# Low parts of the expert weights, taken in five conv steps of VectorE instead of three

## The reference, cut to what matters

```python
def _L0_attn_ref(...):                       # "the conv part" of the kernel
    p = hidden_states @ in_proj_w.T
    h, gate = p[..., :I], silu(p[..., I:])   # I = 256
    h = (causal grouped conv of h, 4 taps) + conv_b
    h = h * gate                             # the gated product
    hn = _layernorm(h, ln_g, ln_b)
    m = silu(hn @ fc_w.T + fc_b) @ cproj_w.T + cproj_b
    return (m + h) @ out_w.T
x = _layernorm(x + _L0_attn_ref(x, ...))     # "the first norm"
...
def _L0_ffn_ref(x, gate_w, w1, w2, w3):      # 8 experts, top 2 of them per token
    scores = softmax(x2d @ gate_w.T); top_scores, sel = top_k(scores, 2)
    for e in range(8):                       # on the rows sent to expert e
        h = silu(xe @ w1[e]) * (xe @ w3[e]); out += h @ w2[e]
x = _layernorm(x + _L0_ffn_ref(x, ...))
```

## Time and profile before

| | |
|---|---|
| time, median of 3 runs | 378.95 us (378.64 to 382.75) |
| the profiled execution | 379.13 us, its span 377.3 us |
| TensorE busy in the span | 330.8 us (88%) |
| VectorE | 262.0 us (69%) |
| ScalarE | 210.4 us (56%) |
| GpSimd | 174.6 us (46%) |
| mean granted clock of TensorE | 0.965 |
| chain that ended last | TensorE 63%, VectorE 10%, issue 5%, ScalarE 3%, GpSimd 3% |

### The profile page before, as it was taken

One profiled execution on the slowest core, in us unless ns is written; L12 is line 12 of the kernel. 1 busy time (PEld: TensorE's weight loads), 2 busy tenths in 40 slices (PEclk: granted clock), 3 DMA queues, 4 the chain that ended last, 5 costly groups with the idle time before them and its releaser, 6 DMA issues.

```text
span 377.3 us, 8518 instructions
## 1 busy us (share of the span) xinstructions
PE 330.8 (88%) x2540; PEld 302.3 (80%) x2540; DVE 262.0 (69%) x857; ACT 210.4 (56%) x430; POOL 174.6 (46%) x234
## 2 busy tenths in 40 slices
PE   4799889966875999999985999999988999999990
PEld 1788778956764999888974788888787999999990
DVE  3558887875872567768774589987796867667741
ACT  2266556735522355445448678887467667667340
POOL 0014577673464345886579666643311342244200
PEclk9899999998897899999999899999999999999996
DMA  8980001021132433322501300000000000000001
GB/s 276 432 341 1 16 29 39 29 66 28 50 87 77 147 99 103 126 58 58 156 23 31 111 2 0 3 3 0 2 3 1 2 14 17 14 14 1 14 16 31
DMA packets 17033, 23.71 MB, mean 63 GB/s; under 512 B 3424, under 2 KB 14176, under 8 KB 16208
## 3 DMA queue, kind: packets, MB, share of 16 engines
q1 hardware_dynamic: 13712, 17.97, 14.5%
q0 software_dynamic: 2272, 4.69, 3.7%
q10 hardware_dynamic: 1008, 0.53, 0.5%
HBM read 17.45 MB, written 6.73 MB: 64 GB/s over the span
## 4 chain that ended last, share of the span: by engine, by line
PE 63%; DVE 10%; issue 5%; ACT 3%; POOL 3%; another core or an unknown queue 2%; DVEq 0%; POOLq 0%; ACTq 0%
PE ps L1958 9%; PE ps L1959 9%; PE ps L1595 8%; PE ps L1597 6%; PE ps L1596 6%; PE ps L1795 5%; PE ps L1903 4%; PE ps L2021 3%; PE ps L1784 3%; PE ps L1918 2%; ACT sb_stage L733 1%; PE ps L1678 1%; PE ps L1930 1%; PE ps L1860 1%
## 5 line engine op out<-in xcount | busy, mean ns | idle before, releaser
L1958 PE MATMUL ps<-sb_w_hi,sb_fh_hi 128*128 128x256 f32 x256 | 63.4, 288 | 1.1 <-DVE sb_w_lo L912 0.6
L1959 PE MATMUL ps<-sb_w_lo,sb_fh_hi 128*128 128x256 f32 x256 | 62.2, 283 | 0.0
L1958 PEld LDWEIGHTS ps<-sb_w_hi,sb_fh_hi 128*128 128x128 f32 x256 | 49.0, 191 | 2.2 <-issue 1.0
L1959 PEld LDWEIGHTS ps<-sb_w_lo,sb_fh_hi 128*128 128x128 f32 x256 | 49.0, 191 | 0.0
L457 POOL DMA_INDIRECT routed<-sb_rows_of,sb_row x32 | 31.7, 991 | 17.5 <-issue 9.2
L1595 PE MATMUL ps<-sb_w_hi,sb_rT_hi 128*128 x78 | 30.7, 393 | 8.8 <-ACT sb_stage L733 6.1
L1795 PE MATMUL ps<-sb_w,sb_stage 128*128 x234 | 33.7, 281 | 2.3 <-issue 1.1
L605 POOL TENSOR_TENSOR sb_w_lo<-sb_x_in,sb_w_hi 128x256 fp32r<-128x256 f32 x24 | 17.5, 757 | 36.9 <-DVE sb_w_hi L1531 36.9
L1795 PEld LDWEIGHTS ps<-sb_w,sb_stage 128*128 128x128 f32 x234 | 29.8, 195 | 3.1 <-issue 3.0
L556 POOL DMA_INDIRECT answers<-sb_stage x24 | 25.0, 1041 | 12.5 <-issue 6.3
L577 POOL TENSOR_TENSOR sb_w_lo<-sb_x_in,sb_w_hi 128x512 fp32r<-128x512 f32 x16 | 20.7, 1293 | 20.4 <-DVE sb_w_hi L1392 20.2
(11 more groups left out here) (304 smaller groups left out, 1045.6 us busy)
## 6 DMA issues: line engine op xcount, KB each, us to landing
sb_stage<-in_w SPq DMA_DIRECT2D x2, 1408.0 KB, 13.0
sb_stage<-routed SPq DMA_DIRECT2D x24, 65.0 KB
sb_w<-in_w SPq DMA_DIRECT2D x1, 1536.0 KB, 17.4
sb_x_in<-in_x_tok SPq DMA_DIRECT2D x1, 1024.0 KB, 8.6
sb_x_in<-in_ff_h SPq DMA_DIRECT2D x1, 1024.0 KB
sb_xT_in<-in_ff_h SPq DMA_DIRECT2D x1, 1024.0 KB
sb_got_first<-answers SPq DMA_DIRECT2D x4, 256.0 KB, 3.1
sb_w<-answers SPq DMA_DIRECT2D x4, 256.0 KB, 3.5
```

The lines of the kernel that those rows point to most:

```text
L1958: mm(dst, w_hi, x_hi, start=start, stop=False)
L1959: last = mm(dst, w_hi, x_lo, start=False, stop=stop and exact)
```

## The change

ScalarE makes the high parts in steps 0 to 4 (two experts, two, two, one, one) where it had steps 0 to 2 (two, three, three). VectorE makes low parts at two places in a step. `LOW_FIRST` puts one between the first norm and the gated product in each of steps 2 to 5 (experts 2, 4, 6, 7). `LOW_LAST` leaves some behind the moments, where all were: two in step 1 as before, one in step 2 (was three), one in step 3 (was three). In sum there are eight as before. GpSimd's memset moves from its step 4 to its step 6, because `moe_lo` reaches 8 only in VectorE's step 5.

```diff
--- before.py
+++ after.py
@@ -44,7 +44,9 @@
 AT_COUNT = AT_RANK + TILES * EXPERTS
 TABLE_STEPS = 16
 SPLIT_AT = (15, 17, 19, 21, 27, 29, 31, 33)
-EXPERTS_AT = {0: (0, 1), 1: (2, 3, 4), 2: (5, 6, 7)}
+EXPERTS_AT = {0: (0, 1), 1: (2, 3), 2: (4, 5), 3: (6,), 4: (7,)}
+LOW_FIRST = {2: 2, 3: 4, 4: 6, 5: 7}
+LOW_LAST = {1: (0, 1), 2: (3,), 3: (5,)}
 
 
 C_IDENT, C_BEFORE, C_KVMASK = 0, P, 2 * P
@@ -480,7 +482,7 @@
                 scatter_some(i - 4, range(2, 4))
                 first_root(i - 2)
                 scatter_some(i - 3, range(0, 2))
-                if i == 4:
+                if i == 6:
                     pool.wait_ge(wt["moe_lo"], EXPERTS)
                     pool.memset(hid[:, :, :], 0.0).then_inc(wt["hid_zero"], 1)
             for i in range(BATCHES):
@@ -1282,8 +1284,10 @@
                     first_norm(i - 2)
                 if i - 2 == PHASE_ENDS[0]:
                     share_tiles(0)
+                if i in LOW_FIRST:
+                    low_part_of_expert(LOW_FIRST[i])
                 gate_and_moments(i)
-                for e in EXPERTS_AT.get(i - 1, ()):
+                for e in LOW_LAST.get(i, ()):
                     low_part_of_expert(e)
                 if i - 2 == PHASE_ENDS[0]:
                     list_tiles(0)
```

## The result

The changed kernel took 373.38 us (median of 4 runs, 372.74 to 376.35), the kernel before 380.15 us in the same comparison (4 runs, 378.64 to 382.75). The ratio is 0.9868, with a 95% interval from 0.9824 to 0.9911. On the 378.95 us from which the prediction started, that is 5.0 us, from 3.4 to 6.7. I had forecast 2.8 us. Measured twice more, on two chips, the ratio was 0.9899 (0.9864 to 0.9933) and 0.9928 (0.9896 to 0.9960), that is 3.8 and 2.7 us. The first comparison alone would have given a wrong size; the profile shows why.

The account below looks back on a forecast made before the run. TensorE's work, about 8 us, was taken as the floor under a step, with VectorE's lateness adding 1.6 us in steps 3 and 4. 1.53 + 1.13 + 0.69 - 0.55 = 2.8 us gave 376.1 us, range 374.7 to 378.3.

Parts of the forecast that it names:

- VectorE's tail, step 3: Two low parts leave the tail of step 2, TensorE's own work becomes the bound, and step 3 gives 1.53 us.
- Step 4: Two low parts leave the tail of step 3; GpSimd's late root limits the gain at x1's transposes to 1.13 us.
- The low parts ahead of the gated product: In steps 2 to 4 gaps of 0.98 to 1.05 us hide a low part of 0.82 us, so cost nothing.
- The memset: Leaving GpSimd's step 4, it ends TensorE's wait of 0.69 us in step 5, and costs nothing in step 6.
- Given back in step 6: GpSimd's root of the first norm comes late again in step 6, so 0.55 us of the gain is lost.
- A scatter beside a low part: GpSimd's scatter in steps 3 and 4 lengthens by 0.2 us, bounds 0 and 0.82 each, left out of the sum.
- The clock: TensorE's low-clock stretches in the expert part may begin or end elsewhere: at most 2 us either way, taken as 0.
- The signs of being wrong: Expert part or what follows changing its length by over 1 us, or a scatter beside a low part taking 1.5 us.
- (A): VectorE's whole relief arrives and low-clock stretches shorten: 3.35 us and up to 1 more, 374.6 to 375.1 us; chance 0.17.
- (B): At the expert part's start, longer low clock or late first-tile rows eat the gain: 378.2 us; chance 0.16 with (D).
- (C): GpSimd becomes the bound through scatters held by low parts, steps over 8.1 us: 379.5 to 381 us; chance 0.05.
- (D): The change does nothing, since the time of steps 3 and 4 comes from TensorE alone; chance 0.16 together with (B).

Follow-up runs that it names:

- all_ahead: Kernel before with each step's own low parts ahead of the gated product, memset left in step 4; ratio to before 1.0006, steps 2 to 7 in 42.27 us.
- twice_ahead: Changed kernel with one extra low part ahead of the gated product in each of steps 2 to 5; ratio to before 1.0009, steps 2 to 7 in 43.52 us.
- once_more_in_tail: Changed kernel with one extra low part behind the moments in each of steps 2 to 5; ratio to before 1.0032, steps 2 to 7 in 43.91 us.
- root_between: Changed kernel with GpSimd's root of the first norm between the two scatters ahead of it; ratio to before 0.9936, steps 2 to 7 in 40.64 us.
- all_in_tails: Changed kernel with all low parts behind the moments, spread over steps 1 to 5; ratio to before 0.9948, steps 2 to 7 in 43.53 us.
- tiny_low_parts: Changed kernel with low parts cut to 8 of 704 columns, the rest zeroed by GpSimd; ratio to before 1.0051, steps 2 to 7 in 41.10 us.

## Why the prediction was right in its mechanism, and what it missed

- **VectorE's tail, step 3: 1.53 us.** Measured 1.60 us (9.65 to 8.05). TensorE took over as the bound, busy for the whole step.
- **Step 4: 1.13 us by the transposes of x1.** The gated product gave 1.28 us (9.66 to 8.38). GpSimd came late as worked out: the first norm waited 0.46 us, where I had 48.6 - 48.07 = 0.5, and TensorE 0.33 us for it.
- **The low parts ahead of the gated product cost nothing.** Right: 0.26 and 0.18 us of the gaps are left in steps 2 and 3. all_ahead and twice_ahead show the cover's limit.
- **The memset, 0.69 us.** The wait of TensorE in step 5 vanished as said. But the size of this term is not shown: alone the move was worth 0.16 us, and no run has the rest of the change without it. The interval of step 5 did not shrink, it grew by 0.25 us (7.86 to 8.11), since the gated product of step 4 came 2.88 us early and that of step 5 2.63. I had 2.6 for the latter. In step 6 the memset cost nothing, but only just: 0.01 us lie between it and the root.
- **Given back in step 6, 0.55 us, so 2.8 us in all.** Measured 2.82, 2.73 and 2.79 us from step 2 to step 7. This sum was the forecast, and it holds to 0.1 us in three pairs of profiles. A small part of that is luck, since two misses cancel: steps 3 and 4 gave 0.22 us more than forecast (2.88 against 2.66), and step 5 gave 0.25 us back where I had 0.06. Step 6 then gained 0.18 us, near the 0.14 that 0.69 - 0.55 leaves.
- **A scatter beside a low part: 0.2 us, bounds 0 and 0.82.** Measured 1.37 us against 1.19: 0.18 us. The size was right, the reason was not. I had taken the scatter to be little held because it mostly writes descriptors. The variants show that a scatter which begins beside low parts waits for their end: 2.17 us with two (1.1 us of them left), 2.97 with three (1.9 us left). In each case the lengthening is what was left of the low parts, less 0.12 to 0.13 us; so it is with the 0.3 us left in the changed kernel, and with the four scatters of 1.22 to 1.60 us in twice_ahead and once_more_in_tail. It cost little because two of the three scatters began 0.18 us ahead of the low part and kept their length, and the third near its end. That was luck of timing. The rule that I weighed, in the Trainium skill ("SBUF — State Buffer", section "SBUF: two separate sides"), agrees with these rows; what was wrong was the 2.3 us that I drew from it, since it took two scatters as held for a whole low part.
- **The clock: 0, bounds 2 us either way.** This is the term that was mis-sized. It was not a term of the change, but of the comparison. In the first pair of profiles it gave most of 1.71 us at the start, where I had not looked at all, and 1.05 us in the first expert tiles. I had asked only whether the change shifts a stretch, and not how far two executions of one kernel differ by such stretches. The runs of the kernel before gave 378.64, 378.95 and 382.75 us, and I took the third for a stray. With 35 runs it is 377.1 to 382.9, so the first result lay by 2 us beyond the effect of the change, and its median, 373.38 us, below the low end of my range, 374.7.
- **The signs of being wrong.** I had named a change of over 1 us in the expert part and behind it. From the gated product of step 7 to the end the first pair differs by 1.72 us (299.44 to 297.72), so by that sign the prediction failed. The second pair differs by 1.0 us the same way, and the third by 1.0 us the other way (290.24 to 291.26). The sign was ill chosen: it can't tell the change from what differs between executions anyway. The other sign, a scatter of 1.5 us, did not come in the changed kernel, but did in three variants.
- **The rivals.** (A), 3.35 us and more, is refuted by the first norm's waits and by the 2.8 us of the conv part, though the first result came nearer to its time than to mine. (Its time was also worked out wrongly: 3.35 us and up to 1 more give 374.6 to 375.6 us.) (B), late rows of the first tile, did not happen here, but it is what root_between ran into. (C) is refuted as to the time, since the kernel is faster in all three comparisons; but its sign, a step over 8.1 us through GpSimd, was there in step 4 (8.38 us), and its mechanism, the held scatter, is real. (D) is refuted by steps 3 and 4, in after and in all_in_tails.

The three ratios, weighted by their intervals, give 0.9904, that is 3.6 us (2.9 to 4.4), a little over the 2.8 us of the conv part. Whether the rest is chance or a weak effect on what follows stays open. The profiles show no second place where the changed kernel is faster in all three pairs.

## What to carry to other kernels

In a ring of engines an instruction costs by its place: ahead of the one that waits anyway it is nearly free up to the length of the wait, and behind it it counts until another engine becomes the bound (here 0.80 of its 0.82 us in steps 3 and 4 of all_in_tails). Measure the gap, and fill it with that much and no more. Look also at what another engine starts beside the moved instruction: a scatter that began beside three low parts took 2.97 us here, and one that began just ahead of a low part kept its 1.03 us. Before an order on a second engine is improved, ask which transfer its last entry releases. And where executions of one kernel differ by as much as the effect, take the effect from the stretch of the profile that the change touches, and let many runs only confirm it.

## What the runs showed of the hardware

In tiny_low_parts GpSimd set 5568 columns to zero at the start:

```profile
6.36 4.74 POOL L455 MEMSET sb_w_lo<- 128x5568 f32 x1
```

VectorE's small copies that began beside it did not end before it did. The memset ahead of them took 0.07 us, the copy of 24 columns 4.66 us:

```profile
6.33 0.07 DVE L959 MEMSET sb_upto<- 128x17 f32 x1
6.46 4.66 DVE L962 COPY sb_first_rows<-sb_const 128x24 f32<-128x24 f32 x1
```

The next two copies took 4.59 and 4.52 us and ended at the same time, 11.1 to 11.3 us, as GpSimd's memset did. The Trainium skill ("SBUF — State Buffer", section "SBUF: two separate sides") says that VectorE in its two-port mode and GpSimd exclude each other for a whole instruction; these rows agree, down to a copy of 24 columns, if these copies run in that mode, which no row shows. In the changed kernel the same three copies took 0.17, 0.17 and 0.29 us. The gated product of step 0 came 3.65 us later than in the kernel before, for an instruction on an engine that had nothing else to do.

GpSimd is held in the same way by VectorE's low parts, which read two operands in SBUF: a scatter that began with 0.3, 1.1 or 1.9 us of low parts still to run took 0.18, 0.98 or 1.78 us longer than the 1.19 us without them.

The second surprise is the clock. In the 6.9 us behind the gated product of step 7 TensorE had the same instructions at the same times, to 0.02 us, in before and after, but over the four microseconds from 6.0 us on its granted clock was 0.59 in the one and 1.00 in the other. The silu of the third expert tile came 1.05 us later in the first. At the start, a stretch at 0.51 took 1.5 us longer than the same work at 1.00.
